# Cross-attention of a decoder layer: taking transposes and weighting in pairs of key pieces

## The chip, the core and the metric

The kernel runs on one core of a Trainium2 chip. The metric is the device time of one execution, in microseconds (us). The three runs of the kernel before gave 2562.75, 2563.09 and 2565.01 us; their median is 2563.09 us.

## What is computed

One decoder layer on x (4 batches of 512 tokens, 256 channels): self-attention, cross-attention and a channel mix, each added to x. The change lies in cross-attention alone. The reference for it, cut to its core (x comes in normalised; all 4 x 512 = 2048 queries of the batch look at all 4 x 1024 = 4096 keys, with 8 heads of 128 channels):

```python
qh = _split_heads(jnp.einsum('bnq,qi->bni', x, Wq))
kh = _split_heads(jnp.einsum('bmc,ci->bmi', context, Wk))
vh = _split_heads(jnp.einsum('bmc,ci->bmi', context, Wv))
sim = jnp.einsum('hid,hjd->hij', qh, kh) * SCALE
mean = jnp.mean(sim, axis=-1, keepdims=True)
sim = (sim - mean) * 1.5 + mean
attn = jax.nn.softmax(sim, axis=-1)
out = jnp.einsum('hij,hjd->hid', attn, vh)
```

## The kernel before

Self-attention and the projections come first. Cross-attention then goes head by head (8), and in each head through 8 groups of 256 queries (two tiles, t = 0 and 1, of 128). A group's work is spread over two steps. In step g, **scores** of group g are computed in 4 chunks of 1024 keys for each tile (items `A`, or `A+` where they already belong to the next group): six matmuls of 512 columns at L1648, since each product is made of three passes over high and low parts. VectorE scales each chunk out of the PSUM tile xs_ps, which has two buffers, and takes its maximum (L1815). ScalarE takes the exponential in chunks (`E`, L1753).

In the same step, the probabilities of group g-1 are turned and weighted with the values, in 16 **pieces** of 256 keys:

- `T` c: TensorE makes four transposes of 128x128 (L1713) into buffer c % 3 of the PSUM tile xt_ps. ScalarE copies the piece to pt_hi, rounded (L1746), and VectorE writes what is left to pt_lo (L1827). pt_hi and pt_lo have three buffers as well.
- `W` c: TensorE makes six matmuls of 256 columns (L1724), which add the piece to xo_ps.

TensorE's waits around them: `T` c, from c = 3, waits until pt_lo of piece c-3 is written, which frees the xt_ps buffer; `W` c waits until pt_lo of piece c is written. ScalarE's copy of piece c waits for `T` c, and from c = 3 for the end of `W` c-3, which frees the pt_hi buffer.

The order of the work is written out by hand, as one list of items for each kind of step. All engines walk the same list, and each does its part of an item or nothing: `W` concerns TensorE alone. The function `with_pieces` (L1351) builds the list: it lays out `T` and `W`, and puts the other items, `extra[c]`, behind piece c. In the usual step (`STEP`) these are chunks of scores behind pieces 0, 2, 4, 6 and 8 for the group itself and behind 12, 14 and 15 for the next, the projection of queries `Q+` behind 7 (six matmuls of 256 columns, L1640), the output projection `out` behind 10 (six matmuls of 256 columns, L1662), and exponentials behind 3 to 6 and 10 to 13. The last step of a head (`STEP_8`) also has the next head's key and value projections (`K+`, `V+`, L1614 and L1631) behind most odd pieces. The last head has its own lists (`LAST_1` to `LAST_8`), which bring in the preparation of the channel mix. In all, 64 steps have pieces.

Of the kernel before, what the change touches and what calls it, by code (L numbers as in the profile page):

```python
# [1352 lines left out]
def with_pieces(extra, ahead=()):  # L1353

    items = list(ahead)
    for c in range(PIECES):
        items.append(("T", c))
        if c >= 2:
            items.append(("W", c - 2))
        items += extra.get(c, [])  # L1360
    return items + [("W", PIECES - 2), ("W", PIECES - 1)]

# [18 lines left out]
AHEAD = {7: [("Q+",)], 12: [("A+", 0, 0)], 14: [("A+", 0, 1)], 15: [("A+", 0, 2)]}  # L1381
OUT = {10: [("out",)]}
STEP_1 = with_pieces(merged(SCORES, EXPS, AHEAD, {5: [("wkv",)], 9: [("wo",)]}))
LAST_1 = with_pieces(merged(SCORES, EXPS, AHEAD, {9: [("wo",)]}))
STEP = with_pieces(merged(SCORES, EXPS, AHEAD, OUT), [("O",)])
STEP_7 = with_pieces(merged(SCORES, EXPS, OUT, {9: [("wq",)], 11: [("K+", 0)], 13: [("K+", 1)], 15: [("Q+",)]}), [("O",)])
STEP_8 = with_pieces({0: [("K+", 2)], 1: [("I",)], 2: [("K+", 3)], 3: [("Q+",)], 4: [("out",)], 5: [("V+", 4)], 6: [("A", 0, 0)],
# [798 lines left out]
```

## Time and profile before

| | |
|---|---|
| median of 3 runs | 2563.09 us |
| the profiled execution, its own time | 2563.48 us |
| its span, first to last instruction | 2561.7 us |
| TensorE (PE) busy | 2515.3 us, 98% |
| VectorE (DVE) busy | 1911.8 us, 75% |
| ScalarE (ACT) busy | 1609.5 us, 63% |

A row of the page gives an engine's busy time and its share of the span. Matmuls are pipelined: each is recorded for longer than the distance to the next, so the pace of TensorE is read from the distances between starts. A row of the timeline merges instructions of one kind that follow each other; its first number is the start of the first of them. A row of waits says which engine stood idle, before which tile and line, until which engine and line had finished.

### The profile page before, as it was taken

Reading aid. Unit: us, or ns where it says so; the run is one execution under the profiler, and the core shown is the slowest. Engines: PE = TensorE matmul, PEld = TensorE weight load, DVE = VectorE, ACT = ScalarE, POOL = GpSimd, SP = SyncE. Lnnn points to the kernel's source line nnn. Section 1 sums busy time; section 2 is a strip of 40 time slices with the busy share of each in tenths; the row PEclk is TensorE's granted clock in tenths of the full one; section 3 lists DMA queues with packets and bytes.
Section 4 is the critical chain, followed back from the end, with each engine's and each line's share of the span. In section 5 each row is a group of like instructions: output and inputs, shape, how many; then the busy total and the mean of one; then the engine's idle time right before and its main releaser. Section 6 shows DMA issues by size and latency. Waiting matters only on the chain. (4 is left out here: it accounts for less than half of the span.)

```text
span 2561.7 us, 47026 instructions
## 1 busy us (share of the span) xinstructions
PE 2515.3 (98%) x17647; PEld 2288.1 (89%) x17647; DVE 1911.8 (75%) x3606; ACT 1609.5 (63%) x3049; POOL 158.3 (6%) x208
## 2 busy tenths in 40 slices
PE   8999989999999999999999999999999999999998
PEld 6899878999899989998999899998999899989997
DVE  5788777777777777777777777777777777777787
ACT  6899746655665655665666566656655665655666
POOL 1344320000000000000000000000000000000013
PEclk9999999999999999999999999999999999999999
DMA  8766441002100120011000300021002100110001
GB/s 246 217 160 153 144 177 34 17 17 92 41 17 19 64 75 18 16 67 67 26 17 11 122 18 17 17 107 34 17 17 92 41 17 21 63 69 18 29 1 34
DMA packets 60637, 155.47 MB, mean 61 GB/s; under 512 B 8848, under 2 KB 22352, under 8 KB 60464
## 3 DMA queue, kind: packets, MB, share of 16 engines
q1 hardware_dynamic: 56464, 140.15, 17.0%
q0 software_dynamic: 3248, 12.72, 1.6%
q8 instruction: 113, 1.85, 0.3%
q14 instruction: 60, 0.49, 0.1%
q10 hardware_dynamic: 752, 0.26, 0.0%
HBM read 125.70 MB, written 27.39 MB: 60 GB/s over the span
## 5 line engine op out<-in xcount | busy, mean ns | idle before, releaser
L1724 PE MATMUL xo_ps<-pt_hi,values 128*128 128x256 f32 x4096 | 949.8, 298 | 1.8 <-DVE pt_lo L1827 1.7
L1746 ACT CAST pt_hi<-xt_ps 128x512 fp32r<-128x512 f32 x1024 | 592.2, 585 | 548.3 <-PE xt_ps L1713 530.2
L1827 DVE TENSOR_TENSOR pt_lo<-xt_ps,pt_hi 128x512 fp32r<-128x512 f32 x1024 | 703.8, 687 | 242.2 <-ACT pt_hi L1746 237.9
L1815 DVE TENSOR_SCALAR_CACHE_REDUCE xprobs<-xs_ps 128x1024 f32<-128x1024 f32 x512 | 626.6, 1224 | 174.5 <-PE xs_ps L1648 169.9
L1724 PEld LDWEIGHTS xo_ps<-pt_hi,values 128*128 128x128 f32 x4096 | 693.3, 188 | 5.4 <-DVE pt_lo L1827 2.6
L1713 PE MATMUL xt_ps<-ident,xprobs 128*128 128x128 f32 x4096 | 603.4, 272 | 0.0
L1753 ACT ACTIVATE xprobs<-xprobs,xneg_max 128x1024 f32<-128x1024 f32 x512 | 591.7, 1156 | 13.4 <-DVE xneg_max L1822 13.4
L1724 PE MATMUL xo_ps<-pt_lo,values 128*128 128x256 f32 x2048 | 570.1, 278 | 0.0
L1713 PEld LDWEIGHTS xt_ps<-ident,xprobs 128*128 128x128 f32 x4096 | 487.9, 140 | 59.9
L1724 PEld LDWEIGHTS xo_ps<-pt_lo,values 128*128 128x128 f32 x2048 | 388.5, 190 | 2.3
L1648 PE MATMUL xs_ps<-k_hi,q_hi 128*128 128x512 f32 x1024 | 328.1, 401 | 0.5
L1648 PE MATMUL xs_ps<-k_lo,q_hi 128*128 128x512 f32 x1024 | 321.5, 395 | 0.0
L1648 PE MATMUL xs_ps<-k_hi,q_lo 128*128 128x512 f32 x1024 | 320.8, 394 | 0.0
L1648 PEld LDWEIGHTS xs_ps<-k_hi,q_lo 128*128 128x128 f32 x1024 | 191.9, 187 | 47.0
L1648 PEld LDWEIGHTS xs_ps<-k_lo,q_hi 128*128 128x128 f32 x1024 | 192.0, 187 | 46.5
L1648 PEld LDWEIGHTS xs_ps<-k_hi,q_hi 128*128 128x128 f32 x1024 | 156.0, 188 | 5.0 <-DVE values L1875 4.0
L1593 POOL TENSOR_SCALAR xprobs<-x,wo_raw 128x256 f32<-128x256 f32 x8 | 9.7, 1213 | 2126.6 <-DVE wo_raw L1321 2126.6
L1759 ACT CAST v_split<-xo_ps 128x256 fp32r<-128x256 f32 x64 | 23.8, 372 | 160.7 <-PE xo_ps L1724 160.7
L836 ACT ACTIVATE probs<-s_ps,neg_max 128x512 f32<-128x512 f32 (+3 forms) x256 | 120.1, 554 | 1.9 <-DVE neg_max L876 1.9
L884 DVE TENSOR_TENSOR spt_lo<-t_ps,values 128x512 fp32r<-128x512 f32 x160 | 103.9, 682 | 20.0 <-ACT values L845 20.0
L1631 PE MATMUL xs_ps<-kv_split,v_split 128*128 128x256 f32 x768 | 101.6, 281 | 7.8 <-DVE values L1875 4.0
L876 DVE TENSOR_REDUCE neg_max<-s_ps 128x2 f32<-128x1024 f32 (+3 forms) x128 | 101.6, 815 | 8.9 <-PE s_ps L754 6.4
(234 smaller groups left out, 2514.7 us busy)
## 6 DMA issues: line engine op xcount, KB each, us to landing
v_split<-ctx_split SPq DMA_DIRECT2D x68, 768.0 KB, 5.7
xq<-x_split SPq DMA_DIRECT2D x64, 512.0 KB, 3.3
values<-rel_split SPq DMA_DIRECT2D x32, 256.0 KB, 3.7
values<-q_split SPq DMA_DIRECT2D x32, 192.0 KB, 4.5
values<-k_split SPq DMA_DIRECT2D x32, 192.0 KB, 4.6
ctx_split<-ctx_out POOLq DMA_DIRECT2D x8, 768.0 KB, 4.1
q_split<-attn_late SPq DMA_DIRECT2D x8, 512.0 KB, 4.0
k_split<-attn_late SPq DMA_DIRECT2D x8, 512.0 KB, 5.5
```

The costliest lines, as they stand in the source:

```text
L836: last = act.activation(probs[:, n % 2, k, TILE_AT[i]:TILE_AT[i] + w], bank[:, c:c + w], ACT.Exp, bias=neg_max[:, n % 2, i, k:k + 1])
L876: last = dve.tensor_reduce(neg_max[:, n % 2, i, :], rows, AX.X, ALU.max, negate=True)
L884: dve.tensor_tensor(pt_lo[:, m % 4, :], t_ps[:, m % 3, :], pt_hi[:, m % 4, :].bitcast(F32), ALU.subtract).then_inc(pt_ready, 1)
L1631: last = pe.matmul(s_ps[:, buf, 2 * XD * t:2 * XD * (t + 1)], blocks[:, b % 4, part, P * t:P * (t + 1)], weights, start=part == 0, stop=pa ...
L1648: last = pe.matmul(s_ps[:, buf, BLK * b:BLK * (b + 1)], q[:, par, P * t:P * (t + 1)], k[:, k0:k0 + BLK], start=m == 0, stop=m == 2)
L1713: last = pe.transpose(t_ps[:, c % 3, GQ * j + P * t:GQ * j + P * (t + 1)], probs[:, 1 - par, t, keys_of(items, c, j)], ident[:])
L1724: last = pe.matmul(o_ps[:, 0:GQ], v[:, vs], pt[:, c % 3, GQ * j:GQ * (j + 1)], start=c == 0 and j == 0 and m == 0, stop=c == PIECES - 1 an ...
L1746: act.copy(pt_hi[:, c % 3, :], t_ps[:, c % 3, :]).then_inc(t_rounded, 1)
L1753: ins = act.activation(probs[:, of, t, cols], probs[:, of, t, cols], ACT.Exp, bias=neg_max[:, of, t:t + 1], accum_out=chunk_sum[:, of, t, ...
L1759: act.copy(o_hi[:], o_ps[:, 0:GQ]).then_inc(o_rounded, 1)
L1815: dve.tensor_scalar(probs[:, par if kind == "A" else 1 - par, t, CHUNK * i:CHUNK * (i + 1)], s_ps[:, buf, :], LOGIT, None, ALU.mult, ALU.m ...
L1827: dve.tensor_tensor(pt_lo[:, c % 3, :], t_ps[:, c % 3, :], pt_hi[:, c % 3, :].bitcast(F32), ALU.subtract).then_inc(t_ready, 1)
```

## The change

One function changes. `with_pieces` used to lay out one transposed piece and one weighted piece in turn; now it lays out two transposed pieces and then the two pieces ahead of them. The lists of all 64 steps are built by it. The extra items keep their place behind `T` c; behind an odd c, from 3 on, they stand behind the two `W`.

```diff
--- before.py
+++ after.py
@@ -1355,8 +1355,8 @@
     items = list(ahead)
     for c in range(PIECES):
         items.append(("T", c))
-        if c >= 2:
-            items.append(("W", c - 2))
+        if c % 2 and c >= 3:
+            items += [("W", c - 3), ("W", c - 2)]
         items += extra.get(c, [])
     return items + [("W", PIECES - 2), ("W", PIECES - 1)]
```

Before, TensorE's part of a usual step reads T0 A T1 T2 W0 A T3 W1 T4 W2 A T5 W3 T6 W4 A T7 W5 Q+ T8 W6 A T9 W7 T10 W8 out T11 W9 T12 W10 A T13 W11 T14 W12 A T15 W13 A W14 W15. Behind the change it reads T0 A T1 T2 A T3 W0 W1 T4 A T5 W2 W3 T6 A T7 W4 W5 Q+ T8 A T9 W6 W7 T10 out T11 W8 W9 T12 A T13 W10 W11 T14 A T15 W12 W13 A W14 W15.

## Rows read from the trace of the kernel before

**Rows 1.** The page: span, engines' busy times and shares, and granted TensorE clock.

```profile
span 2561.7 us, 47026 instructions
...
PE 2515.3 (98%) x17647; PEld 2288.1 (89%) x17647; DVE 1911.8 (75%) x3606; ACT 1609.5 (63%) x3049; POOL 158.3 (6%) x208
...
PEclk9999999999999999999999999999999999999999
```

**Rows 2.** Windows: length, busy us and instructions of PE, PEld, DVE, ACT, POOL; clock; DMA.

```profile
350.00:2487.00 2137.00, 2126.12 (x14983) 1939.03 (x14981) 1576.74 (x2980) 1287.02 (x2379) 11.16 (x16) 1.00 0.12 42
```

**Rows 3.** The page's costliest groups: busy, mean ns of one, idle before, releaser.

```profile
L1724 PE MATMUL xo_ps<-pt_hi,values 128*128 128x256 f32 x4096 | 949.8, 298 | 1.8 <-DVE pt_lo L1827 1.7
...
L1713 PE MATMUL xt_ps<-ident,xprobs 128*128 128x128 f32 x4096 | 603.4, 272 | 0.0
```

**Rows 4.** Waits: total us, times, longest us.

```profile
PEld xs_ps L1631 <- DVE values L1875: 10.1, 13, 2.0
...
PE xo_ps L1724 <- DVE pt_lo L1827: 1.7, 2, 0.8
```

**Rows 5.** Timeline of PE, one usual step: its start, T0, T1 and T2, its end.

```profile
1023.44 0.60 PE L1713 MATMUL xt_ps<-ident,xprobs 128*128 128x128 f32 x4
...
1025.28 1.03 PE L1713 MATMUL xt_ps<-ident,xprobs 128*128 128x128 f32 x8
...
1026.27 0.28 PE L1724 MATMUL xo_ps<-pt_lo,values 128*128 128x256 f32 x1
...
1054.23 0.60 PE L1713 MATMUL xt_ps<-ident,xprobs 128*128 128x128 f32 x4
```

**Rows 6.** Timeline of PE, same step: T7, W5, Q+, T8, W6, A, T9.

```profile
1035.62 0.60 PE L1713 MATMUL xt_ps<-ident,xprobs 128*128 128x128 f32 x4
...
1036.17 0.28 PE L1724 MATMUL xo_ps<-pt_lo,values 128*128 128x256 f32 x1
...
1036.74 0.84 PE L1640 MATMUL xs_ps<-xq,v_split 128*128 128x256 f32 x6
1037.42 0.60 PE L1713 MATMUL xt_ps<-ident,xprobs 128*128 128x128 f32 x4
...
1037.98 0.28 PE L1724 MATMUL xo_ps<-pt_lo,values 128*128 128x256 f32 x1
...
1038.57 0.63 PE L1648 MATMUL xs_ps<-k_hi,q_hi 128*128 128x512 f32 x2
...
1039.97 0.60 PE L1713 MATMUL xt_ps<-ident,xprobs 128*128 128x128 f32 x4
```

**Rows 7.** Timeline of PE, same step: W1 and its end; W13 and its end; start of W14.

```profile
1028.79 0.28 PE L1724 MATMUL xo_ps<-pt_lo,values 128*128 128x256 f32 x1
...
1029.38 0.60 PE L1713 MATMUL xt_ps<-ident,xprobs 128*128 128x128 f32 x4
...
1050.86 0.28 PE L1724 MATMUL xo_ps<-pt_lo,values 128*128 128x256 f32 x1
...
1051.43 0.62 PE L1648 MATMUL xs_ps<-k_hi,q_hi 128*128 128x512 f32 x2
...
1052.82 0.28 PE L1724 MATMUL xo_ps<-pt_hi,values 128*128 128x256 f32 x1
```

**Rows 8.** Timeline of ACT, same step: copy of piece 9, an exponential, copy of piece 15.

```profile
1041.81 0.59 ACT L1746 CAST pt_hi<-xt_ps 128x512 fp32r<-128x512 f32 x1 [0.54 <-PE xt_ps L1713]
1042.29 1.15 ACT L1753 ACTIVATE xprobs<-xprobs,xneg_max 128x1024 f32<-128x1024 f32 x1
...
1051.01 0.59 ACT L1746 CAST pt_hi<-xt_ps 128x512 fp32r<-128x512 f32 x1 [1.47 <-PE xt_ps L1713]
```

**Rows 9.** Timeline of DVE, same step: chunk behind T14, rest of piece 15.

```profile
1050.50 1.23 DVE L1815 TENSOR_SCALAR_CACHE_REDUCE xprobs<-xs_ps 128x1024 f32<-128x1024 f32 x1 [0.24 <-PE xs_ps L1648]
...
1051.65 0.68 DVE L1827 TENSOR_TENSOR pt_lo<-xt_ps,pt_hi 128x512 fp32r<-128x512 f32 x1
```

## The prediction

> **What bounds the kernel now.** I read the page first: TensorE is busy for 98% of the span, VectorE for 75%, ScalarE for 63%, and the clock is granted in full in all 40 slices [rows 1]. Then I cut out the stretch that the change can touch, cross-attention from 350 to 2487 us: TensorE is busy for 2126.1 of 2137.0 us [rows 2]. The reader is to see that almost no wait is left there. The costliest groups say it again: the weighting stood idle for 1.8 us before 4096 of its matmuls, the transposes for none [rows 3]; in the list of waits the weighting waits for pt_lo twice, 1.7 us in all, and the longest total in this stretch is the value projection's 10.1 us at the ends of heads [rows 4]. So TensorE's own pace is the bound. What a new order can give or take is in the distances between matmul starts, and I read those last, in the timeline of one usual step, 1023.44 to 1054.23, so 30.79 us [rows 5].
>
> **The pace, brick by brick.** T1 and T2 (eight transposes) and the first weighting matmul take 1026.27 - 1025.28 = 0.99 us up to the second matmul [rows 5]; T7 with four transposes takes 1036.17 - 1035.62 = 0.55 [rows 6]. So four transposes are 0.44, and 0.11 is left for the weighting matmul: the passage from T to W costs under 0.01. A chunk is 1039.97 - 1038.57 = 1.40 us behind a W [rows 6]; T0 and a chunk together are 1025.28 - 1023.44 = 1.84, again 0.44 + 1.40 [rows 5].
>
> The weighting itself has two paces. Five distances in W5 are 1036.74 - 1036.17 = 0.57 us, 0.114 each; five in W6 are 1038.57 - 1037.98 = 0.59, 0.118 each [rows 6]. Over longer rows: eleven fast distances, W5 and `Q+` together, are 1037.42 - 1036.17 = 1.25, 0.1136 each [rows 6], and the twelve slow distances of W14 and W15 are 1054.23 - 1052.82 = 1.41, 0.1175 each [rows 5, 7]. So a fast W is 0.682, a slow one 0.705, and I count 0.024 between them. Of the 16 in this step six are fast: W0, W5, W7, W9, W11, W13. All six stand behind a chunk (or `out`) and a transposition. W13 is one of them: 1051.43 - 1050.86 = 0.57; W1 stands in the same place and is slow, 1029.38 - 1028.79 = 0.59 [rows 7]. The five behind a W and a T (W2, W4, W8, W10, W12) are all slow, and so are W14 and W15. Neither operands nor sizes differ between them; what came before does. The pace is also handed on within a row of 256-column matmuls: `Q+` behind the fast W5 takes 1037.42 - 1036.74 = 0.68 us [rows 6].
>
> Sum of the step before: 16 T x 0.436 = 6.98; six fast and ten slow W = 4.09 + 7.05 = 11.14; eight chunks x 1.40 = 11.20; `Q+` 0.68; `out` about 0.71; together 30.71. The 0.08 left over of 30.79 is spread over some thirty passages from one kind of work to another, about 0.003 each.
>
> **Removed and added work.** None: the same instructions, DMAs and semaphores. SP's and POOL's queues are passed by nothing, since `W` belongs to TensorE alone and the other engines' lists keep their order.
>
> **Passages.** Per step T to W falls from 14 to 7 and W to chunk from 8 to 1 (W13 to A stays), while T to chunk rises from 1 to 8. That is 7 passages fewer and 7 changed for another kind. At 0.003 to 0.004 each, and the trace's T to A no dearer than its W to A within 0.01, I take 0.03 us saved per step. Bounds: nothing, and 14 x 0.01 = 0.14.
>
> **Paces.** This is the large term, and the trace has no run of T, chunk, T behind a weighting, so I bound it. Best: all 14 W of the seven pairs fast, 8 more than now: 8 x 0.024 = 0.19 saved per step. Worst: none fast, 6 x 0.024 = 0.14 lost. For the value between, I follow what each passage did to the pace in this step. A slow W, then chunk, T: fast in W5, W7, W11, W13. A fast W, then T: slow (W6, W8, W10, W12), and then chunk, T: fast again. If a missing W in between changes nothing, as the length of a run changes nothing, then a fast pair followed by T, chunk, T makes a fast pair again. The pairs that now stand after W0's place (W0 W1 and W2 W3) come out slow by the same bookkeeping, as W1 and W3 do now; the other five, W4 to W13, fast. That is 10 fast of 16 against 6: 4 x 0.024 = 0.10 saved.
>
> **Waits.** T3 comes 0.7 us sooner, at about 4.1 us of the step, and needs pt_lo of piece 0, which now follows T0 (over by 0.6) by copy and rest, 0.59 [rows 8] and 0.68 [rows 9] plus passages, at 2.0. Each odd T stands where the W before it stood, 0.7 sooner. ScalarE's copy of an odd piece now waits for the end of W c-3, which follows T c: 0.6 to 0.7 us later than T's end. Behind that copy stand, in ScalarE's queue, an exponential of 1.15 us in pieces 3 to 6 and 10 to 13, and the next copy; the copy is 0.48 from start to start [rows 8]. Per pair ScalarE needs at most 2 x 1.6 = 3.2 us, TensorE 3.7 with a chunk and 3.0 with `out`; at piece 11 the wait and the backlog cover each other. The tightest place is piece 15: its copy, at 1051.01 before [rows 8], would wait for W12, at about 27.6 us of the step, which is 1051.0; the rest of it runs from 1051.65, behind the chunk that now comes 0.7 sooner [rows 9], and W15, the last six distances before 1054.23, needs it at 1053.5 [rows 5]. Cover: 1.2 us, as now. I cost the waits at nothing; if a cover broke, each 0.1 us per step would be 6.4 us. What would be late next is the next step's T0, for the last exponential: it has over 3 us. In the last head's last step the pieces from 8 on have no chunks, only ScalarE's and VectorE's work for the channel mix, and the cover is small; a loss there comes once, up to 1 us.
>
> **Sum.** Per step -0.10 - 0.03 = -0.13; with 64 steps -8.5 us. `STEP_8` has other extras (a chunk or projection behind nearly every piece), and I take it like the others. The profiled execution took 2563.48 us, 0.4 above the median, so: 2563.48 - 8.5 = 2555.0 us.
>
> **Rivals.** (1) *All pairs fast*: 64 x (0.19 + 0.03) = 14.1 us, 2549. For it: each pair stands behind a chunk and a T, where six of nine W are fast. Against: W1, W3 and W6 stand there too and are slow.
>
> (2) *Order doesn't matter*: the share of fast W stays near six and only passages are saved, 0 to 2 us, 2561.5 to 2563.5. For it: TensorE works 98% of the time through the same list of matmuls. The Trainium skill (TensorE: Matmul & The Clock Gate, "Back-to-back issue gap") has a rule that speaks for this: the distance follows from the column count alone, 262 cycles for 256 columns, which as an estimate is 109 ns, whatever came before. The trace doesn't agree: 114 and 118 ns stand for one and the same instruction [rows 6]. By the rule the sum would be nil.
>
> (3) *Every pair starts slow* and hands the slow pace to its second half: 6 x 0.024 = 0.14 lost, 0.03 regained, 64 x 0.11 = 7.0 us slower, 2570.5. The place is the pair's first matmul, the price 0.024 us per W; it decides when fewer than about five of the 16 W are fast (6 - 0.03 / 0.024). For it: the fast W of before had another W between the T and the chunk ahead of them, which is gone, and W15 to T0 to chunk is the one place where T, chunk follow a W directly, with two T behind. Against: that place gives a fast W0.
>
> **How the numbers follow.** A measurement of this kernel can tell about 0.2%, 5.1 us, from no change, so "faster" begins below 2558.0 and "slower" above 2568.2. The forecast (7 to 12 fast) has 0.40; (1) 0.17; (2) 0.20; (3) with any broken cover 0.23. The range must leave out no more than 0.2: from 2547, (1) with a little more from the passages, to 2572, (3) with a little for a cover. Of the forecast's 0.40 some lies above 2558. Faster: 0.50; within: 0.27; slower: 0.23.
>
> **What would show it.** In the new timeline of a usual step: its length 30.66 us; five distances of 0.57 in W4 to W13 and 0.59 in W0 to W3, W14, W15; T and chunk together 1.84; passages under 0.01; idle time before the weighting and the transposes still under 3 us. The forecast is wrong if distances in the pairs are 0.118 throughout, if TensorE shows waits for pt_lo in the usual step, or if a chunk behind a T takes more than 1.40.

## The result, and the profile after

The changed kernel takes 2576.66 us (median of 5 runs, 2573.41 to 2581.35) against 2563.38 us (5 runs, 2562.75 to 2565.01): ratio 1.0053, with a 95% interval of 1.0042 to 1.0063. It is 13.3 us slower. The forecast was 8.5 us faster, and the range ended at 2572.

The profiled execution took 2581.35 us and spans 2579.6 us, 17.9 more than that of before. The page of the changed kernel, the lines that answer to [rows 1] and [rows 3]:

```profile
span 2579.6 us, 47058 instructions
...
PE 2527.6 (98%) x17647; PEld 2297.3 (89%) x17647; DVE 1912.4 (74%) x3606; ACT 1610.4 (62%) x3049; POOL 158.3 (6%) x208
...
L1724 PE MATMUL xo_ps<-pt_hi,values 128*128 128x256 f32 x4096 | 843.4, 289 | 1.8 <-DVE pt_lo L1827 1.7
```

The page says little. TensorE has the same number of instructions and is busy for 12.3 us more. The weighting's idle time is still 1.8 us, so its waits did not grow. Its busy time even fell, from 949.8 to 843.4 us, which is no gain but comes of how the records overlap. The first matmul behind a T is recorded for 0.36 us in place of 0.28 (it starts 0.03 behind the last transpose), and there are half as many of them: the mean of 4096 falls by 9 ns, 37 us in sum. The rest of the fall is that the two W of a pair stand back to back, so that their records cover each other in part. The time must be found by the starts of T0 in each step. I cut the span there:

| us | before | after | difference |
|---|---|---|---|
| up to the first T0 | 393.9 | 398.2 | +4.3 |
| the 56 usual steps (all but the last of each head) | 1720.9 | 1726.0 | +5.1 |
| seven stretches: STEP_8 to the next head's first T0 | 375.4 | 384.6 | +9.2 |
| the last head's last step and the rest | 71.4 | 70.8 | -0.6 |
| span | 2561.7 | 2579.6 | +17.9 |

The first row is no work of the change, which begins behind it. In the first 50 us this execution had a mean granted clock of 0.90, where the trace of before has 1.00; TensorE did 160 matmuls in them and not 180. Windows of the changed kernel:

```profile
0.00:50.00 50.00, 39.26 (x160) 29.96 (x161) 28.90 (x78) 30.97 (x56) 12.39 (x25) 0.90 0.70 231
```

Without those 4.3 us, the trace is 13.6 us longer, near the 13.3 of the medians. So two things are to be explained: 5.1 us in the usual steps and 9.2 us in the stretches with STEP_8.

**The usual step.** A usual step isn't always the same: steps 3 to 6 of a head, 32 of the 56, have one length and one set of fast W in all eight heads, and rows 5 to 7 are of such a step; steps 1, 2 and 7 have sets of their own. What follows is of one of the 32. Timeline of PE, changed kernel, from T0, then T3 W0 W1 T4, T5 W2 W3 T6, and the next step's T0:

```profile
1032.10 0.60 PE L1713 MATMUL xt_ps<-ident,xprobs 128*128 128x128 f32 x4
...
1036.77 0.28 PE L1724 MATMUL xo_ps<-pt_lo,values 128*128 128x256 f32 x1
...
1038.02 0.60 PE L1713 MATMUL xt_ps<-ident,xprobs 128*128 128x128 f32 x4
1038.37 0.71 PE L1648 MATMUL xs_ps<-k_hi,q_hi 128*128 128x512 f32 x2
...
1039.85 0.60 PE L1713 MATMUL xt_ps<-ident,xprobs 128*128 128x128 f32 x4
...
1040.41 0.28 PE L1724 MATMUL xo_ps<-pt_lo,values 128*128 128x256 f32 x1
...
1041.71 0.60 PE L1713 MATMUL xt_ps<-ident,xprobs 128*128 128x128 f32 x4
...
1045.40 0.87 PE L1640 MATMUL xs_ps<-xq,v_split 128*128 128x256 f32 x6
1046.11 0.60 PE L1713 MATMUL xt_ps<-ident,xprobs 128*128 128x128 f32 x4
...
1063.01 0.60 PE L1713 MATMUL xt_ps<-ident,xprobs 128*128 128x128 f32 x4
```

The step takes 1063.01 - 1032.10 = 30.91 us, 0.12 more than before. Eleven distances of W0 and W1 are 1038.02 - 1036.77 = 1.25 us, the fast pace; those of W2 and W3 are 1041.71 - 1040.41 = 1.30, the slow one. From here to the end of the step every W is slow: 2 of 16 are fast where 6 were [rows 6, 7], and `Q+` behind the slow W5 takes 0.71 in place of 0.68. T4, chunk, T5 starts at 1038.02 and T5 at 1039.85: 1.83, as forecast. So 4 x 0.024 + 0.03 = 0.12: the pace is the whole difference, and nothing is left for passages. Over the 64 steps 125 W are fast; before it was 343.

The second step of a head shows how far back the cause of a pace can lie. Its list is the same in all heads, but in four heads W0 and W1 are fast in it, and in the other four W8 and W9. The four with W8 and W9 are those in whose first step W0 and W1 were fast; in the other four no W was fast in the first step. In steps 3 to 6 all heads agree.

**STEP_8.** Waits in the changed kernel, TensorE's before the key projection:

```profile
PE xs_ps L1614 <- DMA v_split<-ctx_split: 5.5, 6, 1.4
...
PE xs_ps L1614 <- DVE k_lo L1865: 1.7, 3, 0.9
```

Before, the transfer was waited for once, for 0.6 us. Timeline of PE, changed kernel, T1 and T2 of one STEP_8, K+ 3, T3:

```profile
1158.92 1.03 PE L1713 MATMUL xt_ps<-ident,xprobs 128*128 128x128 f32 x8
1160.26 2.57 PE L1614 MATMUL xs_ps<-v_split,kv_split 128*128 128x512 f32 x10 [0.31 <-DMA v_split<-ctx_split]
1162.67 0.60 PE L1713 MATMUL xt_ps<-ident,xprobs 128*128 128x128 f32 x4
```

Eight transposes are over 0.87 us after their start, at 1159.8; K+ 3 starts at 1160.26. Windows of the changed kernel; the last two numbers are the DMA engines' share and GB/s:

```profile
1158.00:1159.00 1.00, 1.00 (x6) 0.78 (x5) 0.42 (x2) 0.64 (x1) 0.00 (x0) 1.00 0.82 299
1159.00:1160.00 1.00, 0.95 (x9) 0.71 (x7) 0.59 (x2) 0.88 (x2) 0.00 (x0) 1.00 0.66 270
1160.00:1161.00 1.00, 0.74 (x3) 0.67 (x4) 1.00 (x2) 0.77 (x2) 0.00 (x0) 1.00 0.09 37
```

The DMA engines fall silent just as K+ 3 starts. In the timeline of PE of the kernel before, the same place has a W0 in it:

```profile
1149.93 1.03 PE L1713 MATMUL xt_ps<-ident,xprobs 128*128 128x128 f32 x8
1150.72 0.36 PE L1724 MATMUL xo_ps<-pt_hi,values 128*128 128x256 f32 x1
...
1151.51 2.49 PE L1614 MATMUL xs_ps<-v_split,kv_split 128*128 128x512 f32 x10
```

K+ 3 started 1151.51 - 1149.93 = 1.58 us after T1. It reads blocks whose load SP issues once K+ 1, in the step before, is done with their buffers. That load had landed in time in six heads of seven, but only just. SP's issues of the loads (L946), kernel before, same place:

```profile
L946 SPq DMA_DIRECT2D v_split<-ctx_split x4: 320/382/437, 1138.3 to 1143.3; - x4
...
DMA to landing us min/median/max: 4.2/5.8/7.9
```

The last of the four transfers was issued at 1143.3 and took the longest, 7.9 us, so it landed at 1151.2, 0.3 us ahead of K+ 3. Over the six heads the cover was 0.2 to 0.6 us. With W0 moved behind T3, K+ 3 could start 0.87 after T1, 0.7 us sooner, and is too early. The seven stretches, 53.4 to 53.5 us each but one before, are now 54.3 to 55.5 and no two alike. Where nothing is waited for in this order (e9 and e10 below), K+ 3 starts 3.56 us behind STEP_8's T0; here it starts 4.11 to 5.21 behind, 7.9 us of waiting in the seven heads.

### The profile page after: what moved, and what is told of

Its sections match the earlier page's. It is cut to its first block and busy times, and to the rows that moved or that the text cites. A ratio compares the mean times of both kernels' runs of the same rounds, so it can differ in the third digit from the quotient of the medians.

```text
span 2579.6 us, 47058 instructions
## 1 busy us (share of the span) xinstructions
PE 2527.6 (98%) x17647; PEld 2297.3 (89%) x17647; DVE 1912.4 (74%) x3606; ACT 1610.4 (62%) x3049; POOL 158.3 (6%) x208
## 5 line engine op out<-in xcount | busy, mean ns | idle before, releaser
L1724 PE MATMUL xo_ps<-pt_hi,values 128*128 128x256 f32 x4096 | 843.4, 289 | 1.8 <-DVE pt_lo L1827 1.7
L1724 PEld LDWEIGHTS xo_ps<-pt_hi,values 128*128 128x128 f32 x4096 | 661.5, 188 | 5.1 <-DVE pt_lo L1827 2.6
L1713 PE MATMUL xt_ps<-ident,xprobs 128*128 128x128 f32 x4096 | 597.8, 272 | 0.5 <-DVE pt_lo L1827 0.5
L1724 PE MATMUL xo_ps<-pt_lo,values 128*128 128x256 f32 x2048 | 571.4, 279 | 0.0
L1713 PEld LDWEIGHTS xt_ps<-ident,xprobs 128*128 128x128 f32 x4096 | 487.3, 140 | 62.0 <-DVE pt_lo L1827 0.8
L1724 PEld LDWEIGHTS xo_ps<-pt_lo,values 128*128 128x128 f32 x2048 | 386.6, 189 | 2.6
L1648 PE MATMUL xs_ps<-k_hi,q_hi 128*128 128x512 f32 x1024 | 357.8, 430 | 0.5
L1631 PEld LDWEIGHTS xs_ps<-kv_split,v_split 128*128 128x128 f32 x768 | 95.2, 188 | 16.1 <-DVE values L1875 10.1
```

The lines of the kernel that those rows point to most:

```text
L1631: last = pe.matmul(s_ps[:, buf, 2 * XD * t:2 * XD * (t + 1)], blocks[:, b % 4, part, P * t:P * (t + 1)], weights, start=part == 0, stop=pa ...
L1648: last = pe.matmul(s_ps[:, buf, BLK * b:BLK * (b + 1)], q[:, par, P * t:P * (t + 1)], k[:, k0:k0 + BLK], start=m == 0, stop=m == 2)
L1713: last = pe.transpose(t_ps[:, c % 3, GQ * j + P * t:GQ * j + P * (t + 1)], probs[:, 1 - par, t, keys_of(items, c, j)], ident[:])
L1724: last = pe.matmul(o_ps[:, 0:GQ], v[:, vs], pt[:, c % 3, GQ * j:GQ * (j + 1)], start=c == 0 and j == 0 and m == 0, stop=c == PIECES - 1 an ...
```

## The experiments

All kernels build their lists with one function that has the orders as options; its longer text shifts the lines of cross-attention by 11 to 15, so that L1614 is L1625 or L1629 there, and L1713 is L1724, L1726 or L1728. In e3, e4 and e12 `STEP_8` and `LAST_8` keep the order of before. I read each trace by the same cut as above.

| kernel | ratio (95%) | usual steps | seven stretches |
|---|---|---|---|
| before | | 1720.9 | 375.4 |
| after | 1.0053 (1.0042 to 1.0063) | 1726.0 | 384.6 |
| e1, pairs but in STEP_8 | 1.0023 (1.0013 to 1.0032) | 1726.0 | 375.6 |
| e2, pairs in STEP_8 alone | 1.0022 (1.0013 to 1.0032) | 1720.6 | 382.0 |
| e3, T T W W chunk | 1.0049 (1.0033 to 1.0065) | 1733.4 | 376.1 |
| e4, T T chunk W W | 1.0141 (1.0120 to 1.0163) | 1757.8 | 377.2 |
| e5, pairs, K+ 3 later | 1.0054 (1.0037 to 1.0071) | 1726.2 | 384.7 |
| e6, one and one, one transpose twice | 1.0016 (1.0005 to 1.0026) | 1725.5 | 377.7 |
| e7, one and one, K+ 3 sooner | 1.0032 (1.0018 to 1.0045) | 1720.6 | 384.2 |
| e8, one and one, chunks behind odd pieces | 1.0060 (1.0043 to 1.0076) | 1735.6 | 375.8 |
| e9, pairs, K+ 0 sooner | 1.0025 (1.0015 to 1.0035) | 1726.6 | 376.3 |
| e10, pairs, K+ 1 sooner | 1.0027 (1.0015 to 1.0039) | 1726.3 | 376.4 |
| e11, pairs, one transpose twice | 1.0086 (1.0066 to 1.0107) | 1732.0 | 384.2 |
| e12, first pair only, K+ 1 sooner | 0.9980 (0.9971 to 0.9989) | 1718.5 | 373.8 |

The sums are of one trace each. The last row of the cut above, the last head's last step and the rest, takes 70.8 to 71.8 us in half of the fourteen traces and 73.0 to 73.3 in the other half, with no relation to the order, so a difference of 2 us between two spans says nothing by itself.

### The two halves

```diff
-STEP_8 = with_pieces({...}, [("O",)])
+STEP_8 = with_pieces({...}, [("O",)], order="one")
```

> STEP_8 alone goes back to one and one; all other steps stay in pairs. Theory (two causes: the pace of the weighting in the usual steps, 1726.0 us against 1720.9 in the two traces, and a new wait of K+ 3 in STEP_8 for its blocks, which makes the seven stretches from STEP_8's first transpose to the next head's first one 384.6 us in place of 375.4): those seven stretches come back to about 376 us, no wait before K+ 3 is left but the one that was there before (0.8 us in the last of them), and the time is about 5 us over the kernel before, 2568. Rival (the pace costs it all, STEP_8's included, and the wait is only where it shows): the stretches stay at 382 or more and the time stays at 2573 or more. Rival (the pairs in the usual steps cost nothing): the time is that of the kernel before, 2563.

Measured 2569.8 us against 2563.27 of before. The stretches are back at 375.6 and the usual steps stay at 1726.0, as in the changed kernel. The 6.5 us are 1.5 more than I expected; the trace has 5.3 of them in these two rows and 1.7 in the last part.

```diff
+with_pieces(..., order="one")            # all lists
-STEP_8 = with_pieces({...}, [("O",)])
+STEP_8 = with_pieces({...}, [("O",)], order="two")
```

> The other half: pairs in STEP_8 alone, one and one in all other steps. Theory: usual steps take 1721 us in sum as before (30.79 us each), the seven stretches with STEP_8 take 383 to 385 us, time 8 to 9 us over the kernel before, 2572. Rival (the wait needs the usual steps' new order as well): under 3 us over the kernel before. The two halves should add up to the whole, 13 us, within 2 us.

Measured 2569.75 us: 6.5 over the kernel before, as is e1, and less than the 8 to 9 that I expected. The halves add up to 13.0 of the 13.3 us. The wait in STEP_8 is smaller here than in the changed kernel (the stretches grow by 6.6, not 9.2, and I expected 383 at least), but it needs no pairs in the usual steps. K+ 3 starts 3.74 to 5.07 us behind T0 there, 5.4 us of waiting in sum where the changed kernel has 7.9: the transfers landed sooner in this trace.

### What makes K+ 3 wait

```diff
 # all lists one and one
-STEP_8: {0: [("K+", 2)], 1: [("I",)],            2: [("K+", 3)], 3: [("Q+",)], ...
+STEP_8: {0: [("K+", 2)], 1: [("I",), ("K+", 3)],                 3: [("Q+",)], ...
```

> The kernel before (one and one) with K+ 3 of STEP_8 moved ahead by T2 and W0, so about 1.15 us earlier, with nothing paired. Theory (the load's landing sets the time of K+ 3, at 4.1 to 5.2 us behind T0 of STEP_8 in the traces so far): K+ 3 starts as late as ever and TensorE waits 1 to 2 us in each of seven heads; the seven stretches grow from 375.4 to 382 to 388 us, the time to 2570 to 2576. Rival (the wait came from VectorE's or ScalarE's queue behind the pairs): no wait, 2563.

Measured 2572.86 us, and stretches of 54.6 to 55.2, 384.2 in sum: nearly the whole of the changed kernel's loss in STEP_8, with nothing paired. The move is larger than that of the pairs, 1.15 us against 0.7; but K+ 3 starts 4.23 to 4.81 us behind T0, so the landing sets it. Waits of this kernel:

```profile
PE xs_ps L1625 <- DMA v_split<-ctx_split: 6.6, 6, 1.4
```

The other way round, pairs with K+ 3 late:

```diff
-STEP_8: {0: [("K+", 2)], 1: [("I",)], 2: [("K+", 3)], 3: [("Q+",)], ...
+STEP_8: {0: [("K+", 2)], 1: [("I",)],                 3: [("K+", 3), ("Q+",)], ...
```

> Pairs everywhere, as in the changed kernel, but in STEP_8 the item K+ 3 is moved from behind T2 to behind W0 and W1, about 1.9 us later. Theory (K+ 3 comes too early for its blocks, whose transfer is started only once K+ 1 is done; in the changed kernel it waits 0.5 to 1.8 us in each of seven heads): the wait is gone, the seven stretches with STEP_8 take 376 to 377 us in place of 384.6, the time is 2569, as with STEP_8 in the old order. Rival (the pairs in STEP_8 cost the time in their pace or in waits elsewhere): the stretches stay above 380 and the time above 2573.

My theory was half right. The transfer is not waited for any more, and the stretches differ by 0.02 us between heads. But they are 54.95 each, and the time is no better. Waits of e5:

```profile
PEld xo_ps L1735 <- DVE pt_lo L1838: 5.1, 11, 1.0
PEld xs_ps L1673 <- DVE k_lo L1876: 4.6, 7, 0.7
```

W1 comes before VectorE has written pt_lo of piece 1 (it is still at the chunk of K+ 2), and `out` waits for VectorE to be done with the late K+ 3. K+ 3 can't simply be moved; its blocks have to be there sooner.

```diff
-STEP_7: {..., 9: [("wq",)],            11: [("K+", 0)], 13: [("K+", 1)], 15: [("Q+",)]}
+STEP_7: {..., 9: [("wq",), ("K+", 0)],                  13: [("K+", 1)], 15: [("Q+",)]}
```

> Pairs everywhere, as in the changed kernel; in STEP_7 the item K+ 0 is moved from behind piece 11 to behind piece 9, about 3 us sooner (K+ 1 stays behind 13). K+ 0 starts the load of the first two blocks, K+ 1 that of the next two, which K+ 3 reads. Theory (in the changed kernel the second load is late because both loads, 3.1 MB, share the DMA engines from the end of K+ 0 on): the first load is out of the way, the second lands sooner, the variable wait before K+ 3 (0.5 to 1.8 us in each of seven heads) shrinks to 0.5 us or less, the seven stretches with STEP_8 take 376 to 379 us and the time is 2568 to 2571. Rival (the second load alone is as slow as that): the wait stays above 0.5 us in most heads, stretches over 381.

```diff
-STEP_7: {..., 9: [("wq",)], 11: [("K+", 0)], 13: [("K+", 1)], 15: [("Q+",)]}
+STEP_7: {..., 9: [("wq",)], 11: [("K+", 0)], 12: [("K+", 1)], 15: [("Q+",)]}
```

> Pairs everywhere, as in the changed kernel; in STEP_7 the item K+ 1 is moved from behind piece 13 to behind piece 12, about 1.9 us sooner (K+ 0 stays behind 11). Theory of shared DMA engines: the second load starts 1.9 us sooner but then runs beside the first; the landing gains under 1 us, waits of 0 to 1 us are left before K+ 3, stretches 379 to 382 us. Rival (the start of the second load alone counts): the landing gains the full 1.9 us and no wait is left, stretches 376 to 377. If K+ 0 and K+ 1 so close to each other make TensorE wait for VectorE in STEP_7, that shows in the usual steps' sum, above 1727 us.

Both bring the stretches to 53.75 to 53.78 us, alike in all heads, and the list of waits names no transfer before L1625 in either. The times are 2569.24 and 2569.2 us: what the pairs cost in pace remains. In e9, K+ 1, which starts the second load, was not moved; only the first load was. The last transfer was issued 3.86 us ahead of STEP_8's T0, as in the changed kernel, but landed 1.8 to 2.8 us behind T0, where there it landed 4.0 to 5.1 behind. So the two loads hinder each other. In e10 I had expected that the sharing would leave a wait; none is left, and there the rival was right that an earlier start is enough: issued 1.8 us sooner, the last transfer landed 1.2 to 2.8 us behind T0. Waits of e10, all that is left before the key projection, none of them in STEP_8's place:

```profile
PEld xs_ps L1625 <- DVE k_lo L1876: 1.7, 2, 1.1
PE xs_ps L1625 <- DVE k_lo L1876: 1.0, 2, 0.9
```

### What sets the pace

```diff
 # usual steps; the item behind an even piece is moved
-T4 chunk T5 W2 W3
+T4 T5 W2 W3 chunk      # e3
+T4 T5 chunk W2 W3      # e4
```

> In the usual steps T T W W chunk: the item behind an even piece is moved behind the pair. STEP_8 and the last head's LAST_8 as before the change. Theory (the pace of a W is set by what TensorE did just before, and nothing else in its surroundings): the paces change against both kernels though all sizes stay the same; a row chunk, T, T gave the fast pace for W0 in the kernel before (where the chunk itself followed a T), so there may be up to 14 fast W in a step, at best 30.6 us; at worst all slow, 30.95 us. Rival (the pace goes with the position of the piece or with what ScalarE and VectorE do beside it): W5, W7, W9, W11, W13 are fast or slow as in one of the two kernels whatever the order. No wait of the weighting in the usual steps by either.

2576.79 us; a step takes 31.05. Two W are fast, and they are W4 and W5 (in 55 of the 56 usual steps): in the steps 3 to 6 of neither kernel was W4 fast, and W0 and W1 are slow now. I was wrong on the waits. T3 is transposed so soon after T2 that W1 comes before pt_lo of piece 1 is written. The list of waits doesn't show it; the distances from W0's last matmul to W1's second do, 0.185 and 0.229 us where 0.118 each would be even, so 0.18 us per step.

> In the usual steps T T chunk W W: the item behind an even piece is moved between the two transposed pieces and the pair. STEP_8 and LAST_8 as before the change. Theory (the pace is set by what TensorE did just before): a W that follows a chunk directly was slow in both kernels (W14 in each of the usual steps), so nearly all W are slow, 0.118 per distance, and a step takes 30.9 to 31.0 us. Rival (position or neighbours on other engines): several W fast, and a step of 30.8 or less.

2600.86 us. No W is fast in 48 of the 56 usual steps, as the theory said (the seventh step of a head has W14 and W15 fast, in most heads W12 and W13 too). But a step takes 31.44 us, because of a new wait that I had not seen: with `Q+`, two transposes and the chunk so close, TensorE comes to the chunk before its xs_ps buffer is free. Waits of e4:

```profile
PEld xs_ps L1659 <- DVE xprobs L1826: 26.5, 48, 0.8
```

Then the smallest change of all, in the kernel before:

```diff
 elif kind == "T":
+    if c == 4:
+        pe.transpose(<first transpose of the piece, same operands and result>)
```

> The kernel before (one and one) with one thing added: the first transpose of piece 4 is made twice, same operands and result, 0.109 us per step. Nothing moves by more than that on any engine. Theory (the pace of a W depends on what TensorE's stream held just before, down to single matmuls): the places of the fast W change behind piece 4 (before: W0, W5, W7, W9, W11, W13), so the step isn't simply 30.79 + 0.109 = 30.90 us, but up to 0.12 more or less. Rival (the pace goes with the piece, its addresses, or what ScalarE and VectorE read at the time): the same W are fast, and a step takes 30.90 us.

2569.08 us. In steps 3 to 6 of a head W3 is fast now, W1 and W2 slow as before, W5 and so on fast as before; over all steps 404 W are fast in place of 343. Timeline of PE, e6, a usual step: the added transpose, W2, chunk, T5, W3, T6:

```profile
1061.88 0.27 PE L1723 MATMUL xt_ps<-ident,xprobs 128*128 128x128 f32 x1
1061.99 0.60 PE L1726 MATMUL xt_ps<-ident,xprobs 128*128 128x128 f32 x4
...
1062.55 0.28 PE L1737 MATMUL xo_ps<-pt_lo,values 128*128 128x256 f32 x1
...
1063.14 0.63 PE L1659 MATMUL xs_ps<-k_hi,q_hi 128*128 128x512 f32 x2
...
1065.10 0.28 PE L1737 MATMUL xo_ps<-pt_lo,values 128*128 128x256 f32 x1
...
1065.67 0.38 PE L1726 MATMUL xt_ps<-ident,xprobs 128*128 128x128 f32 x2
```

W2: 1063.14 - 1062.55 = 0.59. W3: 1065.67 - 1065.10 = 0.57, where it was 0.59. Piece, buffers and addresses are the same, and so is the work of the other engines, shifted by 0.11 us. The step takes 30.89 us, which by itself could not be told from the rival's 30.90; the set of fast W tells it. The same done to the changed kernel:

> The changed kernel with the first transpose of piece 4 made twice (as was done to the kernel before). Theory (what went before sets the pace, and a row T, chunk, T, W, W behind a slow pair gives a slow pair again): W0 and W1 stay fast, W2 and W3 may change, W4 to W13 stay slow or come back to slow within a few pieces; a step takes 30.91 + 0.11 = 31.02 us, less at most 0.05. Rival (one more transpose is enough to leave the slow cycle for good): six or more fast W behind it and a step under 30.90 us.

2584.68 us, 31.03 a step, with W0 and W1 fast in steps 3 to 6 and no other: the slow cycle of T, chunk, T, W, W is entered again at once. In the second step of each head W2 and W3 are the fast ones, at 31.01 us.

```diff
-SCORES = {0: ..., 1: ..., 2: [("A", 1, 0)], 4: [("A", 1, 1)], 6: [("A", 1, 2)], 8: [("A", 1, 3)], 9: [("M", 1)]}
+SCORES = {0: ..., 1: ..., 3: [("A", 1, 0)], 5: [("A", 1, 1)], 7: [("A", 1, 2)], 9: [("A", 1, 3), ("M", 1)]}
```

> The kernel before (one and one) with the four chunks of scores behind pieces 2, 4, 6, 8 of the usual steps put behind 3, 5, 7, 9. Theory (alternation: a slow W, a chunk and a T give a fast W, a fast W and a T give a slow one, except in the first pieces, where W1 to W4 were slow in a row): the W that follow chunk, T are now W2, W4, W6, W8 and may be fast from W2 on, 7 to 9 fast W in a step in place of 6, so a step of 30.70 to 30.77 us and 2558 to 2562. Rival (the pace goes with the position): six fast W at their old places, 30.79. With both, if a chunk or an exponential comes too late, waits show and the time is over 2564.

2579.97 us; a miss as an improvement. W2 and W4 are fast together in 30 of the 56 usual steps and both slow in 21, changing from step to step; W5 and W7, which now follow a W and a T, are slow in every one. So the pace didn't stay with the position. But the order didn't give what the theory asked either: W6 and W8 follow a chunk and a T now and are slow in all steps but one, and over all steps 249 W are fast, fewer than the 343 of before. But a step takes 31.04 to 31.09 us, because T3 and W1 now follow W0 without a chunk between, and pt_lo of piece 1 isn't there: 9.5 us of waits in 44 places.

```profile
PEld xo_ps L1735 <- DVE pt_lo L1838: 9.5, 44, 1.0
```

### A version made from the rows

What the traces showed, written as passages: T0, chunk, T1, T2, chunk, T3 gives a fast W0 and W1 (after, in 47 of the 56 usual steps); a fast W and a T give a slow W (before); a slow W of that kind, chunk and T give a fast W (before). Put together, they ask for a pair at the start of the step and for one and one from there on:

```diff
-        if c >= 2:
-            items.append(("W", c - 2))
+        if c >= 3:
+            items += [("W", 0), ("W", 1)] if c == 3 else [("W", c - 2)]
         items += extra.get(c, [])
-STEP_7: {..., 9: [("wq",)], 11: [("K+", 0)], 13: [("K+", 1)], 15: [("Q+",)]}
+STEP_7: {..., 9: [("wq",)], 11: [("K+", 0)], 12: [("K+", 1)], 15: [("Q+",)]}
```

> One and one, except that W0 waits for T3 and is taken with W1: T0 chunk T1 T2 chunk T3 W0 W1 T4 W2 chunk T5 W3 and so on, in the usual steps; STEP_8 and LAST_8 as before the change, and K+ 1 behind piece 12 in place of 13. Theory (the passages read in the runs so far hold wherever they occur: behind T0 chunk T1 T2 chunk T3 the first W is fast, as in the changed kernel; fast, T, slow; slow, chunk, T, fast, as in the kernel before): W0, W1, W3, W5, W7, W9, W11, W13 are fast, 8 of 16 in place of 6, a usual step takes 30.74 to 30.75 us in place of 30.79, the sum of the usual steps is about 1718 us; with the last wait before K+ 3 gone (0.8 us) the span is 3 to 4 us under that of the kernel before, ratio 0.9985. Rival (the pace can't be foretold from the rows seen): another set of fast W, a step of 30.79 or more, and no gain.

2558.62 us (11 runs) against 2564.39, ratio 0.9980 with an interval of 0.9971 to 0.9989: faster than both kernels. W0, W1, W3, W5, W7, W9, W11 and W13 are fast in steps 3 to 6 of every head, all eight named and no other. In the other usual steps the passages don't foretell so well. In the second step, which has the same list, W0 and W1 are slow in all eight heads, behind T0, chunk, T1, T2, chunk, T3 as well, and the step takes 30.80 us as before; the first and the seventh have six fast W in most heads, W0 and W1 among them. Timeline of PE, e12, a usual step: W0 and W1, T4, W2, chunk, T5, W3:

```profile
1057.18 0.28 PE L1739 MATMUL xo_ps<-pt_lo,values 128*128 128x256 f32 x1
...
1058.43 0.60 PE L1728 MATMUL xt_ps<-ident,xprobs 128*128 128x128 f32 x4
...
1058.99 0.28 PE L1739 MATMUL xo_ps<-pt_lo,values 128*128 128x256 f32 x1
...
1059.58 0.63 PE L1663 MATMUL xs_ps<-k_hi,q_hi 128*128 128x512 f32 x2
...
1060.98 0.60 PE L1728 MATMUL xt_ps<-ident,xprobs 128*128 128x128 f32 x4
...
1061.54 0.28 PE L1739 MATMUL xo_ps<-pt_lo,values 128*128 128x256 f32 x1
1061.65 0.39 PE L1739 MATMUL xo_ps<-pt_hi,values 128*128 128x256 f32 x2
```

W0 and W1: 1058.43 - 1057.18 = 1.25 for eleven distances. W2: 1059.58 - 1058.99 = 0.59. W3 begins with 0.11. The usual steps take 1718.5 us in sum, 2.4 less than before, 30.75 each in steps 3 to 6; the stretches are 373.8, 1.6 less; half of it is the seventh stretch, 0.8 us longer than the others before, whose wait K+ 1's new place removes. The two edits weren't measured apart: of the 5.8 us in the medians (2.8 to 7.4 by the interval) the traces give 4.0, 2.4 of them in the usual steps, where the pair is.

## Why the prediction was wrong

**What held.** TensorE's pace bounds the kernel; the two paces, their 0.024 us, and that a row of 256-column matmuls hands the pace on (both halves of a pair agree in every usual step, and `Q+` follows W5). T, chunk together takes 1.83 to 1.84. No wait of the weighting was added in the usual steps; ScalarE's later copies of odd pieces cost nothing. The rival that order doesn't matter fell: the orders tried for the same matmuls have from none to eight fast W per step. The rule beside it was read too widely. The Trainium skill (TensorE: Matmul & The Clock Gate, "Back-to-back issue gap") gives the 262 cycles for an isolated matmul, and says that in a stream of weight loads and matmuls both set the spacing. Here each matmul has its own weight load (17647 of either), and the spacing is 114 or 118 ns.

**Passages**: sized at 0.03 us saved per step. The step's 0.12 is used up by four W and `Q+`; the saving was about nil.

**Paces: the step that failed first.** The sentence "If a missing W in between changes nothing, as the length of a run changes nothing, then a fast pair followed by T, chunk, T makes a fast pair again" was an assumption, and 0.10 of the forecast 0.13 us per step stood on it. The trace of before had no such passage behind a fast W. (Behind a slow one it had W15, T0, chunk, T1, T2, W0, which the prediction left out where it says that there is no such run; W0 is fast there in steps 3 to 7 and slow in steps 1 and 2.) The changed kernel shows it: fast W0 W1, T4, chunk, T5, slow W2 W3, and slow to the end of the step. The bookkeeping named W0 to W3 slow and W4 to W13 fast; W0 and W1 came out fast, W4 to W13 slow, and it was right on W2 and W3 alone. So 2 of 16 were fast and not 10. In its place stands what rival (3) says of six of the seven pairs: they start slow and stay slow. That its 0.11 us per step is so near the measured 0.12 is luck in part: it had the first pair slow too, which would cost 0.05 more, and 0.03 regained from passages, which didn't come, nor did it count the 0.03 that `Q+` lost. The loss is what e1 isolates, 6.5 us in the measured time (5.1 in the traces' usual steps).

I gave rival (3) 0.23 and the assumption 0.40. The trace of before spoke for the rival: in none of its 64 steps does a fast W follow a fast W, 343 cases. Two of them are in the step that the prediction read, with more than a T between: W1 is slow behind the fast W0, a chunk and T3, and W6 is slow behind the fast W5, `Q+` and T8.

**STEP_8: the step that failed second, and the larger error.** "`STEP_8` has other extras, and I take it like the others." The working of the waits followed pt_lo, pt_hi and the buffers of xs_ps, and it said of T3 that it comes 0.7 us sooner; it never said so of the chunk behind T2, which is K+ 3 in STEP_8, and never looked up what that chunk waits for. It also said "SP's and POOL's queues are passed by nothing", which is true of the lists and misses that TensorE can come sooner than SP's transfer lands. e7 shows this wait without any pairs (8.1 us, 2572.86 - 2564.73), e9 and e10 take it away with the pairs kept, by 7.5 us against the changed kernel (2576.66 - 2569.2). In the kernel before, the cover of this load could have been read off: 0.2 to 0.6 us in six of the seven heads, less than the 0.7 by which K+ 3 was to come sooner, and in the last it was already used up, with 0.6 us of waiting for the transfer in that one place. Other traces with `STEP_8` in the old order show how thin it was: in e6, K+ 3 starts 4.43 to 4.86 us behind T0 in all seven heads, where it starts at 4.36 if nothing is waited for.

Neither failure alone would have taken the time out of the range (e1 and e2 are at 2570); together they did.

**Still open.** Why a 256-column matmul has two paces, and what in the stream picks one. e6 excludes piece and address by themselves for W3, and makes the neighbours on other engines unlikely; it doesn't name the cause. That steps 3 to 6 agree in all heads, though the changed kernel's stretches between the heads differ by up to 1.2 us, speaks against something that runs by a clock of its own beside the kernel; this is argued, not tested. Open too is why the same transfer, issued at the same place, lands 4.0 to 5.1 us behind STEP_8's T0 in the changed kernel's trace and 3.6 to 4.9 in e2's; this difference is that between their stretches.

## What to carry to other kernels

When an order is changed on an engine that is the bound, list every item that comes sooner, not only those that are moved, and for each the event it waits for, transfers included; an item that arrives sooner by 0.7 us needs 0.7 us of cover, and one place in the old trace where that cover is gone is the warning. Where the new order makes a sequence that the old trace doesn't hold, don't extend a pattern over it: one look at the new sequence costs little, and a forecast built of sequences that were all seen (e12) came out matmul for matmul in steps 3 to 6 of each head. It failed in the second step of each, so read more than one step of a kind, and ask whether the pattern holds in all of them.

## What the hardware showed that was not expected

The same matmul of 256 columns, with its weight load, is spaced 0.1136 or 0.1175 us apart, at a granted clock of 1.00 in both cases, and the spacing holds through a row of matmuls of that width. It depends on TensorE's stream before it: one more transpose of 0.109 us ahead of W2 (e6) leaves W2 slow and makes W3, a chunk and a T later, fast. The last few items aren't enough to foretell it: steps with one and the same list have different sets, by which step they are of the head (before: W0 slow and W3 fast in the second, the reverse from the third on) or even by the head (after, second step: W0 and W1 in four heads, W8 and W9 in four, by what the first step was). By order alone steps 3 to 6 had none (e4), two (after, e3), six (before) or eight (e12) fast W; the 0.024 us between a fast and a slow W makes 0.2 us of a 30.8 us step, about 0.6%, between none and eight.
